# A four-block transformer kernel on one core: moving the context-maximum steps, a pair's low parts and one table load inside the first two stages

## The chip, the cores and the metric

The kernel runs as one launch on one core of a Trainium2 chip. The metric is the device time of that core in microseconds (us). Three runs of the kernel before took 817.12, 817.11 and 817.55 us; the median is 817.12 us.

## What is computed

The input `x` is 4 batches of 512 tokens of 512 values (2048 tokens, sixteen tiles of 128). Four blocks follow each other, each a residual step over a layer norm:

```
x = x + matmul(quant_1x128(layernorm(x)), quant_128x128(ctx_2048))        # stage a
x = x + down(silu(gate(ln(x)) * gate_s) * (up(ln(x)) * up_s)) * down_s    # stage b, inner size 1408
x = x + softmax_attention(ln(x), ctx_2048, mask)                          # stage c
x = x + ternary FFN with Hadamard transforms and 8-bit rounding           # stage d, inner size 2048
```

For stage a both operands are rounded to 8-bit floats and scaled back. The context of each batch is a 512x512 matrix in sixteen 128x128 blocks; each block has one scale, which comes from the largest absolute value in the block:

```
amax = max(abs(wb), over the block);  safe = maximum(amax, 1e-6)
q = (wb * (448 / safe)).astype(float8_e4m3fn);  wdq = q * (safe / 448)
```

## The kernel before

Stages a and b run together. The sixteen tiles go in eight pairs ("groups" g = 0 to 7). In group g TensorE runs stage b's gate and up products for the pair 2g, 2g+1 in eleven chunks c = 0 to 10 (`C0`), of 16 matmuls of 128x256 each (`gate_up_b`, L1340). Between the chunks, at chunk numbers that are written out by hand, stand the steps of stage a for the next pair, n0 = 2g+2 and n1 = 2g+3: `a_turn` (four transposes of the quantized tile, L1307) and `a_product` (eight fp32 matmuls with the context, L1312). After the chunks come `b_down(2g)`, the turns of the next pair's normed tiles (`b_turn`), and `b_down(2g+1)`. ScalarE and VectorE have `b_group` functions of their own, with the same chunk numbers. Each engine runs its own list in the order written; semaphores alone tie the engines together.

The steps that the change touches:

- A chunk's hidden values: ScalarE `b_silu` (L503) waits for the chunk; VectorE `b_hidden` (L922) waits for the silu; ScalarE `b_high` (L509) and VectorE `h_low` (L929) split the result in two fp16 parts. Chunk n of TensorE waits for `b_hidden` of chunk n-2 (`wait(pe, b_h_r, n - 1)`, L1342), since two PSUM banks take turns.
- Stage a for tile j: ScalarE `a_scale` (L468), VectorE `a_grids` and `a_rounding`, ScalarE `a_back` (L476, writes what `a_turn` turns), TensorE `a_turn`, ScalarE `a_evac` (L484), TensorE `a_product`, VectorE `a_residual`.
- The context of batch e (e = 1, 2, 3; batch 0 is done ahead of the groups): `context_max(e)` on VectorE (L789, one reduce of 128x2048), `max_turn(e)` on TensorE (L1322, one transpose into PSUM bank 2), `context_top(e)` on VectorE (two small operations, L793), `max_spread(e)` on TensorE (L1329, spreads the sixteen maxima over all partitions), `context_scales(e)` on VectorE (L799), then four times `context_scaled` on ScalarE (L449, four ACTIVATEs each), `context_grid` and `context_rounding` on VectorE (two operations each), and `context_back` on ScalarE. `context_scaled(e, b)` waits for `context_scales(e)`. Batch 1 is handled in groups 0 and 1, batch 2 from group 1 on, batch 3 from group 3 on.
- At a group's end: ScalarE copies the turned tiles out (`b_evac(n0)`, `b_evac(n1)`, L497), VectorE subtracts to get their low parts (`b_low`, L869). TensorE's next group waits for both low parts (`pe.wait_ge(b_xl_r, 2 * g + 2)`, L1364). VectorE's `b_down(2g)` (L945) is the scaling of the down product and the residual addition, two operations of 128x512.
- The first `Silu` on ScalarE stands at group 0, chunk 0.

The next stages, c and d, follow on TensorE behind group 7; stage c's context loads wait for `a_add`, stage d's weight loads for `b_add` and for their roundings.

Of the kernel before, what the change touches and what calls it, by code (L numbers as in the profile page):

```python
# [5 lines left out]
T, D, B, S2 = 2048, 512, 4, 512  # L6
# [19 lines left out]
def fused_blocks(nc, x, ctx_t, ctx_n, mask, gate_t, up_t, down_t, gate_s, up_s, down_s,  # L26
# [4 lines left out]
    ACT = mybir.ActivationFunctionType  # L31
# [3 lines left out]
    with ExitStack() as ctx:  # L35
# [411 lines left out]
        def _(act):  # L447
# [68 lines left out]
            def b_group(g):  # L516
                n0, n1, more = 2 * g + 2, 2 * g + 3, g + 1 < PAIRS
                odd, e, following = g % 2 == 1, (g + 2) // 2, (g + 3) // 2
                sums = (0, 0, 3, 5, 8, 10, 13, 16)
                for c in range(C0):  # L520
                    b_silu(g, c)
                    if c >= 1:
                        b_high(g, c - 1)
                    if more:
                        if c == 2:
                            a_back(n0)
                        if c == 4:
                            a_evac(n0)
                            a_scale(n1)
                        if c == 7:  # L530
                            a_back(n1)
                        if c == 8:
                            a_evac(n1)
                        if g == 0 and 6 <= c < 10:
                            context_scaled(1, c - 6)
                        if g == 1 and c in (3, 5):
                            context_back(1, 2 + c // 5)
                        if g in (3, 5) and c == 0:
                            context_back(e, 3)
                        if c in (0, 6, 9):  # L540
                            k = sums[g] + (0, 6, 9).index(c)
                            if k < sums[g + 1]:
                                weight_sums(k)
                    elif c == 6:
                        act.wait_ge(valid_ps, 1)
                        nc.scalar.activation(valid[:, :], bank(2)[:, 0:B], ACT.Copy).then_inc(valid_r, 1)
                b_high(g, C0 - 1)
                if more:
                    if odd and following < B:
                        for b in range(KD):  # L550
                            context_scaled(following, b)
                    elif g in (2, 4):
                        for b in range(3):
                            context_back(e, b)
                    elif g == 0:
                        context_back(1, 0)
                    if n0 + 2 < NT:
                        a_scale(n0 + 2)
                    b_evac(n0)
                    b_evac(n1)  # L560
                    if g == 0:
                        context_back(1, 1)
# [17 lines left out]
            nc.scalar.activation(ds_bc[:, :], bank(7), ACT.Copy).then_inc(ds_r, 1)  # L580
            a_evac(1)
            a_scale(2)
            b_evac(0)
            b_evac(1)
            act.wait_ge(row_in, 64)
# [179 lines left out]
        def _(dve):  # L765
# [187 lines left out]
            def b_group(g):  # L953
                n0, n1, more = 2 * g + 2, 2 * g + 3, g + 1 < PAIRS
                odd, e, following = g % 2 == 1, (g + 2) // 2, (g + 3) // 2
                for c in range(C0):
                    if c == 0 and g:
                        b_down(2 * g - 1)
                    b_hidden(g, c)
                    if c >= 1:  # L960
                        h_low(g, c - 1)
                    if more:
                        if c == 0:
                            a_grids(n0)
                        if c == 1:
                            a_rounding(n0)
                        if c == 2:
                            a_stats(n1)
                        if c == 3:
                            a_norm(n1)  # L970
                        if c == 5:
                            a_grids(n1)
                        if c == 6:
                            if g == 0:
                                context_scales(1)
                            a_rounding(n1)
                        if c == 7:
                            a_residual(n0)
                            b_stats(n0)
                        if c == 9:  # L980
                            b_norm(n0)
                        if g == 0:
                            if c == 2:
                                context_max(1)
                            if c == 4:
                                context_top(1)
                            if c == 8:
                                context_grid(1, 0)
                            if c == 10:
                                context_grid(1, 1)  # L990
                                context_rounding(1, 0)
                        elif g == 1 and c in (2, 4):
                            context_rounding(1, 1 + c // 2)
                        elif not odd and e < B:
                            if c in (4, 6, 8):
                                context_grid(e, c // 2 - 2)
                                context_rounding(e, c // 2 - 2)
                        if odd and following < B:
                            if c == 6:
                                context_max(following)  # L1000
                            if c == 9:
                                context_top(following)
                        if g == 6 and c == 6:
                            mask_rows()
                    elif c == 2:
                        weight_scales()
                h_low(g, C0 - 1)
                if odd and following < B:
                    context_scales(following)
                if more:  # L1010
                    a_residual(n1)
                    b_stats(n1)
                    if n0 + 2 < NT:
                        a_stats(n0 + 2)
                    b_norm(n1)
                    if n0 + 2 < NT:
                        a_norm(n0 + 2)
                    if g == 0:
                        context_rounding(1, 1)
                        dve.wait_ge(ds_r, 1)  # L1020
                    elif not odd and e < B:
                        context_grid(e, 3)
                    b_low(n0)
                    b_down(2 * g)
                    b_low(n1)
                    if g == 0:
                        context_grid(1, 2)
                        context_grid(1, 3)
                    elif not odd and e < B:
                        context_rounding(e, 3)  # L1030

            for g in range(PAIRS):
                b_group(g)

# [262 lines left out]
        def _(pe):  # L1297
# [63 lines left out]
            def b_group(g):  # L1361
                n0, n1, more = 2 * g + 2, 2 * g + 3, g + 1 < PAIRS
                odd, following = g % 2 == 1, (g + 3) // 2
                pe.wait_ge(b_xl_r, 2 * g + 2)  # L1364
                for c in range(C0):
                    gate_up_b(g, c)
                    if more:
                        if c == 4:
                            a_turn(n0)
                        if c == 6:  # L1370
                            if g == 0:
                                max_spread(1)
                            a_product(n0)
                        if c == 8:
                            a_turn(n1)
                        if c == 10:
                            a_product(n1)
                        if g == 0 and c == 4:
                            max_turn(1)
                        if odd and following < B and c == 8:  # L1380
                            max_turn(following)
                        if odd and following < B and c == 9:
                            max_spread(following)
                    elif c == 4:
                        pe.wait_ge(mask_r, 2)
                        M(bank(2)[:, 0:B], one_f, vrow[:, :], start=True, stop=True).then_inc(valid_ps, 1)
                if g == 0:
                    pe.wait_ge(dn_in, 16)
                    pe.wait_ge(ds_r, 1)
                b_down(2 * g)  # L1390
                if more:
                    b_turn(n0)
                    b_turn(n1)
                else:
                    c_body(-1, 1)
                b_down(2 * g + 1)
# [282 lines left out]
```

## Time and profile before

| what | value |
|---|---|
| median of three runs | 817.12 us |
| the profiled execution, its own time | 815.84 us |
| its span in the trace | 814.0 us (1.84 us lie around it) |
| TensorE busy | 733.8 us, 90% of the span |
| VectorE busy | 609.0 us, 75% |
| ScalarE busy | 421.4 us, 52% |
| GpSimd busy | 261.5 us, 32% |
| mean granted TensorE clock | 0.98 of full |

Rows of the trace give a start in us from the span's start, a duration in us, the engine and line, the operation with what it writes and reads, the count, and in brackets how long the engine stood idle before it and what ended that wait. PE is TensorE (PEld its weight loads), DVE is VectorE, ACT is ScalarE, POOL is GpSimd, SP the engine that issues loads. The groups of stage b begin in the trace at 46.28, 90.58, 133.06, 171.42, 215.53, 253.88, 293.39 and 331.74 us.

### The profile page before, as it was taken

What the parts mean: (1) busy time and instruction counts of PE and PEld (TensorE: products, weight loads), DVE (VectorE), ACT (ScalarE), POOL (GpSimd) and SP (SyncE); (2) the same over time, 40 slices, a digit from 0 to 9 for tenths busy, and PEclk for the clock granted to TensorE, in tenths of its full rate; (3) what the DMA queues carried; (4) which work ended last, traced back from release to release, by engine and by line L of the source; (5) the groups of instructions that cost most, each with busy time, mean ns of one, the idle gap of its engine ahead of it and who ended that gap; (6) DMA issues with size and microseconds to landing.
All of it is one profiled execution on the core that took longest, in us unless ns stands there. A gap on an engine that the chain in (4) does not pass through costs nothing. (4 is left out here: it accounts for less than half of the span.)

```text
span 814.0 us, 13263 instructions
## 1 busy us (share of the span) xinstructions
PE 733.8 (90%) x4443; PEld 449.2 (55%) x4480; DVE 609.0 (75%) x1308; ACT 421.4 (52%) x930; POOL 261.5 (32%) x164
## 2 busy tenths in 40 slices
PE   1579989998999999999999999769999999999947
PEld 0256656666666676754444444345656556555644
DVE  6667877976697677455878865987887888887864
ACT  3536566655665645322122123345777666677645
POOL 3000100000000000000000000498888788888840
PEclk9989999999999999999999999999999999999969
DMA  8950122112111211742333200000000000000001
GB/s 195 268 219 1 40 74 95 40 39 79 31 49 40 78 40 30 282 138 103 122 114 143 103 1 0 1 0 15 14 14 14 13 14 26 13 13 13 14 13 40
DMA packets 24646, 51.71 MB, mean 64 GB/s; under 512 B 2066, under 2 KB 4114, under 8 KB 23572
## 3 DMA queue, kind: packets, MB, share of 16 engines
q1 hardware_dynamic: 21684, 45.96, 16.7%
q0 software_dynamic: 2480, 4.33, 3.0%
q10 hardware_dynamic: 432, 0.79, 0.3%
q8 instruction: 28, 0.46, 0.2%
q14 instruction: 22, 0.18, 0.1%
HBM read 51.20 MB, written 4.19 MB: 68 GB/s over the span
## 5 line engine op out<-in xcount | busy, mean ns | idle before, releaser
L1346 PE MATMUL ps<-arena 128*128 128x256 f16 x1408 | 165.8, 277 | 7.0 <-DVE arena L926 3.4
L1346 PEld LDWEIGHTS ps<-arena 128*128 128x128 f16 x1408 | 137.7, 99 | 35.1 <-DVE arena L926 9.1
L1469 PE MATMUL ps<-arena 128*128 128x512 bf16 x484 | 117.2, 379 | 5.2 <-DVE arena L1122 3.6
L406 POOL TENSOR_TENSOR arena<-arena 128x1024 f32<-128x1024 f32 x42 | 101.5, 2416 | 40.8 <-DVE arena L1131 37.6
L1303 PE MATMUL ps<-I,arena 128*128 128x128 f32 x576 | 82.1, 284 | 31.9 <-ACT arena L481 15.1
L407 POOL TENSOR_TENSOR arena<-arena 128x1024 f32<-128x1024 f32 x42 | 101.1, 2406 | 0.0
L1303 PEld LDWEIGHTS ps<-I,arena 128*128 128x128 f32 x576 | 69.2, 146 | 57.2 <-issue 22.1
L354 POOL TENSOR_TENSOR rstd_a<-ve_a,mhalf 128x1 f32<-128x1 f32 x32 | 19.6, 611 | 250.2 <-DVE ve_a L777 244.0
L354 POOL TENSOR_TENSOR rstd_b<-ve_b,mhalf 128x1 f32<-128x1 f32 x32 | 17.6, 550 | 204.8 <-DVE ve_b L777 204.8
L507 ACT ACTIVATE arena<-ps,gs 128x256 f32<-128x256 f32 x88 | 41.1, 467 | 80.0 <-PE ps L1346 80.0
L926 DVE SCALAR_TENSOR_TENSOR arena<-ps,us,arena 128x256 f32<-128x256 f32 x88 | 42.3, 480 | 51.1 <-ACT arena L507 50.9
L1357 PE MATMUL ps<-arena 128*128 128x512 f16 x352 | 78.6, 379 | 0.0
L1469 PEld LDWEIGHTS ps<-arena 128*128 128x128 bf16 x512 | 48.7, 98 | 52.3 <-issue 2.7
L1122 DVE SCALAR_TENSOR_TENSOR arena<-ps,f_sm,arena 128x512 f32<-128x512 f32 x64 | 48.0, 750 | 34.4 <-ACT arena L637 33.4
L637 ACT ACTIVATE arena<-ps,f_sm 128x512 f32<-128x512 f32 x64 | 44.0, 688 | 47.8 <-PE ps L1469 47.6
L1319 PE MATMUL ps<-arena 128*128 128x512 f32 x128 | 60.3, 616 | 0.8 <-issue 0.8
L1415 PE MATMUL ps<-arena 128*128 (+1 forms) x128 | 59.2, 605 | 0.0
L1555 PE MATMUL ps<-arena 128*128 128x512 bf16 x247 | 56.9, 379 | 2.2 <-ACT arena L662 1.7
L1357 PEld LDWEIGHTS ps<-arena 128*128 128x128 f16 x352 | 34.4, 98 | 41.9 <-issue 4.0
L1430 PE MATMUL ps<-arena 128*128 (+1 forms) x128 | 57.5, 592 | 0.0
L606 ACT ACTIVATE arena<-ps,c_sm 128x512 f32<-128x512 f32 x16 | 11.0, 688 | 85.3 <-DVE c_sm L1063 85.3
L656 ACT ACTIVATE arena<-ps 128x512 f32<-128x512 f32 x56 | 30.4, 600 | 34.8 <-PE ps L1534 34.7
(128 smaller groups left out, 1184.3 us busy)
## 6 DMA issues: line engine op xcount, KB each, us to landing
arena<-in_ctx_t SPq DMA_DIRECT2D x7, 1024.0 KB, 5.3
arena<-in_wg_t SPq DMA_DIRECT2D x16, 256.0 KB, 3.4
arena<-in_wu_t SPq DMA_DIRECT2D x16, 256.0 KB, 4.0
arena<-in_wd_t SPq DMA_DIRECT2D x16, 256.0 KB, 4.1
arena<-in_ctx_n SPq DMA_DIRECT2D x4, 1024.0 KB, 7.5
arena<-in_wg_t SPq DMA_DIRECT2D x4, 1024.0 KB, 5.0
arena<-in_wu_t SPq DMA_DIRECT2D x4, 1024.0 KB, 4.8
arena<-in_wd_t SPq DMA_DIRECT2D x4, 1024.0 KB, 5.2
```

Of the source, the lines that this page charges most:

```text
L406: nc.gpsimd.tensor_tensor(b[:, :, 0, :], a[:, :, 0, :], a[:, :, 1, :], ALU.add).then_inc(d_bfp, 1)
L407: nc.gpsimd.tensor_tensor(b[:, :, 1, :], a[:, :, 0, :], a[:, :, 1, :], ALU.subtract).then_inc(d_bfp, 1)
L637: nc.scalar.activation(d_sil[n % 2], bank(2 * (n % 2)), ACT.Silu, scale=f_sm[:, u, 4:5]).then_inc(d_sil_r, 1)
L1122: V.scalar_tensor_tensor(HA[u][:, D * n:D * n + D], bank(2 * (n % 2) + 1), f_sm[:, u, 5:6], d_sil[n % 2], ALU.mult, ALU.mult).then_inc(d_h ...
L1303: last = nc.tensor.transpose(dst[:, b, :], src[:, b * P:b * P + P], eye_sb)
L1319: last = M(bank(5), a_xT[u][:, b, :], wdq[:, e % 2, b, :], start=(b == 0), stop=(b == KD - 1))
L1346: last = M(bank(n % 2)[:, 2 * P * i:2 * P * i + 2 * P], W[:, b, c * P:c * P + P], part[:, b, at:at + 2 * P], start=(b == 0 and part is xhT ...
L1357: last = M(bank(6 + j % 2), part[:, c, at:at + P], dW[:, c, :], start=(c == 0 and part is hh), stop=(c == C0 - 1 and part is hl))
L1415: last = M(bank(2 + u), c_xT[u][:, b, :], ctxs[:, bass.ds(B - 1 - e, 1), 0, b, :].rearrange("p a m -> p (a m)"), start=False, stop=(b == K ...
L1430: last = M(bank(6 + w), c_pT[w][:, b, :], ctxs[:, bass.ds(B - 1 - e, 1), 1, b, :].rearrange("p a m -> p (a m)"), start=(b == 0), stop=(b = ...
L1469: last = M(bank(2 * (n % 2) + i), d_qT[u][:, b, :], W[:, b, D * n:D * n + D], start=(b == 0), stop=(b == KD - 1))
L1555: last = M(bank(down_bank(j)), yqT[:, c, :], Wd[:, c, :], start=(c == 0), stop=(c == C1 - 1))
```

## The change

Six things are changed, all in the order of work; no arithmetic is added but one dummy `Silu` over one column.

1. `context_max(1)` stands ahead of group 0 on VectorE, instead of in chunk 2.
2. The rest of batch 1's chain in group 0 comes earlier: `max_turn` at chunk 0 (was 4), `max_spread` at 2 (was 6, ahead of `a_product`), `context_top` at 0 (was 4), `context_scales` at 2 (was 6), `context_scaled` at chunks 3, 5, 6, 9 (was 6 to 9), `context_grid(1, 0)` at 4 (was 8), `context_rounding(1, 0)` at 8 (was 10).
3. `a_turn(n1)` on TensorE and `a_evac(n1)` on ScalarE stand at chunk 9 instead of 8, in groups 0 to 6.
4. In groups 1 and 3 `max_spread(following)` stands at chunk 10, behind `a_product(n1)`, instead of at chunk 9.
5. `b_low(n1)` on VectorE stands directly behind `b_low(n0)`, ahead of `b_down(2g)`.
6. A `Silu` over one column into `b_sil[0]` stands ahead of ScalarE's `b_evac(0)`, with its wait for the small loads.

```diff
--- before.py
+++ after.py
@@ -529,10 +529,10 @@
                             a_scale(n1)
                         if c == 7:
                             a_back(n1)
-                        if c == 8:
+                        if c == 9:
                             a_evac(n1)
-                        if g == 0 and 6 <= c < 10:
-                            context_scaled(1, c - 6)
+                        if g == 0 and c in (3, 5, 6, 9):
+                            context_scaled(1, (3, 5, 6, 9).index(c))
                         if g == 1 and c in (3, 5):
                             context_back(1, 2 + c // 5)
                         if g in (3, 5) and c == 0:
@@ -580,6 +580,8 @@
             nc.scalar.activation(ds_bc[:, :], bank(7), ACT.Copy).then_inc(ds_r, 1)
             a_evac(1)
             a_scale(2)
+            act.wait_ge(row_in, 64)
+            nc.scalar.activation(b_sil[0][:, 0:1], gs[:, 0:1], ACT.Silu)
             b_evac(0)
             b_evac(1)
             act.wait_ge(row_in, 64)
@@ -971,8 +973,6 @@
                         if c == 5:
                             a_grids(n1)
                         if c == 6:
-                            if g == 0:
-                                context_scales(1)
                             a_rounding(n1)
                         if c == 7:
                             a_residual(n0)
@@ -980,15 +980,16 @@
                         if c == 9:
                             b_norm(n0)
                         if g == 0:
+                            if c == 0:
+                                context_top(1)
                             if c == 2:
-                                context_max(1)
+                                context_scales(1)
                             if c == 4:
-                                context_top(1)
+                                context_grid(1, 0)
                             if c == 8:
-                                context_grid(1, 0)
+                                context_rounding(1, 0)
                             if c == 10:
                                 context_grid(1, 1)
-                                context_rounding(1, 0)
                         elif g == 1 and c in (2, 4):
                             context_rounding(1, 1 + c // 2)
                         elif not odd and e < B:
@@ -1021,14 +1022,15 @@
                     elif not odd and e < B:
                         context_grid(e, 3)
                     b_low(n0)
+                    b_low(n1)
                     b_down(2 * g)
-                    b_low(n1)
                     if g == 0:
                         context_grid(1, 2)
                         context_grid(1, 3)
                     elif not odd and e < B:
                         context_rounding(e, 3)
 
+            context_max(1)
             for g in range(PAIRS):
                 b_group(g)
 
@@ -1368,18 +1370,18 @@
                         if c == 4:
                             a_turn(n0)
                         if c == 6:
-                            if g == 0:
-                                max_spread(1)
                             a_product(n0)
-                        if c == 8:
+                        if g == 0 and c == 2:
+                            max_spread(1)
+                        if c == 9:
                             a_turn(n1)
                         if c == 10:
                             a_product(n1)
-                        if g == 0 and c == 4:
+                        if g == 0 and c == 0:
                             max_turn(1)
                         if odd and following < B and c == 8:
                             max_turn(following)
-                        if odd and following < B and c == 9:
+                        if odd and following < B and c == 10:
                             max_spread(following)
                     elif c == 4:
                         pe.wait_ge(mask_r, 2)
```

## Rows read from the trace of the kernel before

**Rows 1.** The page: busy time and share of each engine.
```profile
PE 733.8 (90%) x4443; PEld 449.2 (55%) x4480; DVE 609.0 (75%) x1308; ACT 421.4 (52%) x930; POOL 261.5 (32%) x164
```
**Rows 2.** Busy time in stretches: start:end, length, engines, granted clock, DMA share, GB/s.
```profile
46.20:420.00 373.80, 358.40 (x2173) 233.80 (x2173) 271.26 (x625) 189.09 (x537) 22.15 (x37) 0.99 0.25 81
```
**Rows 3.** TensorE's waits: line, releaser: total us, times, longest us.
```profile
PE ps L1303 <- ACT arena L481: 15.1, 9, 9.7
...
PE ps L1331 <- DVE cmx_diag L797: 5.4, 3, 2.3
...
PE ps L1346 <- DVE arena L926: 3.4, 5, 1.0
...
PE ps L1346 <- DVE arena L872: 2.5, 2, 1.5
```
**Rows 4.** Timeline of TensorE in group 0 and at the start of group 1.
```profile
59.24 0.28 PE L1327 MATMUL ps<-I,cmx 128*16 128x128 f32 x1 [1.00 <-DVE cmx L791]
...
61.95 1.92 PE L1346 MATMUL ps<-arena 128*128 128x256 f16 x16 [0.40 <-DVE arena L926]
...
71.60 0.66 PE L1303 MATMUL ps<-I,arena 128*128 128x128 f32 x4 [0.28 <-ACT arena L481]
...
90.58 9.18 PE L1346 MATMUL ps<-arena 128*128 128x256 f16 x80 [1.02 <-DVE arena L872]
```
**Rows 5.** Timeline of VectorE in group 0.
```profile
51.73 0.48 DVE L926 SCALAR_TENSOR_TENSOR arena<-ps,us,arena 128x256 f32<-128x256 f32 x1 [5.60 <-ACT arena L507]
...
56.92 2.27 DVE L791 TENSOR_REDUCE cmx<-arena 128x16 f32<-128x2048 f32 x1
```
**Rows 6.** The issue of batch 1's context load on SP's queue.
```profile
26.18 0.40 SPq L292 DMA_DIRECT2D arena<-in_ctx_t  x1
```
**Rows 7.** All three context loads of L292: from issue to landing.
```profile
DMA to landing us min/median/max: 7.7/10.3/11.9
```
**Rows 8.** A stretch of group 0, columns as in rows 2.
```profile
52.00:54.00 2.00, 2.00 (x21) 1.80 (x19) 1.85 (x6) 0.78 (x2) 0.00 (x0) 1.00 0.15 51
```
**Rows 9.** Timeline of ScalarE around group 0's start.
```profile
42.28 0.60 ACT L501 ACTIVATE arena<-ps 128x512 f16<-128x512 f32 x1 [7.65 <-PE ps L1303]
...
49.93 1.28 ACT L507 ACT_TABLE_LOAD   x1 [4.52 <-PE ps L1346]
```
**Rows 10.** Timeline of VectorE at group 0's end.
```profile
80.45 0.68 DVE L859 TENSOR_TENSOR X<-X,ps 128x512 f32<-128x512 f32 x1
...
89.84 0.68 DVE L872 TENSOR_TENSOR arena<-ps,arena 128x512 f16<-128x512 f32 x1
```
**Rows 11.** Timeline of TensorE in groups 1 and 3.
```profile
117.18 0.39 PE L1331 MATMUL ps<-cmx_diag,ones 16*128 16x16 f32 x2 [2.32 <-DVE cmx_diag L797]
117.50 1.92 PE L1346 MATMUL ps<-arena 128*128 128x256 f16 x16
119.26 3.60 PE L1319 MATMUL ps<-arena 128*128 128x512 f32 x8
...
197.97 0.39 PE L1331 MATMUL ps<-cmx_diag,ones 16*128 16x16 f32 x2 [2.32 <-DVE cmx_diag L797]
198.29 3.44 PE L1346 MATMUL ps<-arena 128*128 128x256 f16 x16
```
**Rows 12.** A stretch of group 3, columns as in rows 2.
```profile
199.00:200.00 1.00, 1.00 (x6) 0.72 (x5) 0.00 (x0) 0.00 (x0) 0.00 (x0) 0.50 0.47 117
```
**Rows 13.** Timeline of ScalarE at group 1's end.
```profile
121.77 4.78 ACT L454 ACTIVATE arena<-arena,cinv 128x128 f32<-128x128 f32 x16 [0.86 <-DVE cinv L803]
128.51 1.28 ACT L473 ACTIVATE arena<-arena,a_sm 128x128 f32<-128x128 f32 x4 [1.97 <-DVE a_sm L839]
```
**Rows 14.** The same stretch on VectorE.
```profile
132.24 0.68 DVE L872 TENSOR_TENSOR arena<-ps,arena 128x512 f16<-128x512 f32 x1
```
**Rows 15.** Stage d: TensorE's two longest waits.
```profile
549.42 3.60 PE L1452 MATMUL ps<-H,arena 128*128 128x512 f16 x8 [5.28 <-DVE arena L1104]
...
782.96 1.94 PE L1303 MATMUL ps<-I,arena 128*128 128x128 f32 x8 [8.14 <-DVE arena L1192]
```

## The prediction

> **What bounds the kernel now.** I read the busy shares first [rows 1]: TensorE is the fullest engine, 90%. That is a mean over four stages, so I took the stretch that the change touches, from group 0's start to the end of stage b [rows 2]: of 373.80 us TensorE works 358.40. At most 15.4 us of waiting can be had there, plus what a lowered clock costs; VectorE (271.26) and ScalarE (189.09) have room on average. Then TensorE's waits by releaser [rows 3], and the timeline, to place each. Inside groups 0 to 7 they are few: waits for `a_back` at the second turn of each pair, for `context_top` at `max_spread`, for `b_hidden` at a chunk, for the low parts at a group's start, and once for `context_max`. As TensorE is otherwise back to back, each microsecond of wait removed there moves everything behind it, unless something else is late next.
>
> **Batch 1's maxima, group 0.** `context_max(1)` holds VectorE from 56.92 for 2.27 us [rows 5]. Behind it TensorE stands 1.00 us at `max_turn`, and 0.40 us at chunk 6, whose `b_hidden` is queued behind the reduce [rows 4]. Ahead of group 0 VectorE stands idle 5.60 us before its first `b_hidden` at 51.73 [rows 5]; the reduce takes 2.27 of these, so it costs nothing if the context has landed. Its load was issued at 26.18 [rows 6] and the slowest of the three such loads took 11.9 us [rows 7]: landed by about 38.5 (26.18 + 0.40 + 11.9), 7.6 us before VectorE gets there at 46.1. The loosest bound is the end of the traffic, which has ebbed by 52 [rows 8]; landing only then would hold back the first `b_hidden` by some 52 + 2.3 - 51.7 = 2.6 us. I take zero, as the landing row is the load's own.
> `max_turn` at chunk 0 finds the maxima made (about 48.4, against a chunk that ends at 49.9, when the first silu's wait ends [rows 9]). `max_spread` at chunk 2 finds `context_top` done: VectorE has it behind `b_hidden(0,0)` and `a_grids`, about 52.3, and chunk 2, which can't begin before that `b_hidden` ends at 52.2, ends after 54. Both small matmuls were there before. The clock is still at its lower level near 50, as it returns to 1.00 only in the stretch from 52 [rows 8]; the turn's 0.28 us may grow by 0 to 0.28, and I estimate 0.1, since part of it is latency.
> Next in line on VectorE is `b_hidden(0,3)`. Without the reduce it follows at about 57.3 instead of 59.11 (0.45 us of `context_scales` now stand in between), before chunk 5 wants it near 59. On ScalarE `context_scaled(1,0)` now stands in chunk 3: four ACTIVATEs, 4.78/4 = 1.2 us [rows 13]. It must not hold up silu 4; by my step-by-step list it ends at 58.9 and the chunk's matmuls at 58.8, so it costs 0.1 of a margin near 1 us. The later ones (chunks 5, 6, 9) stand beside chunks of 1.84 us (9.18/5 [rows 4]) or an `a_product` of 3.60 [rows 11]. Gain: 1.00 + 0.40 - 0.1 = 1.3 us. Bounds: 1.4 if all is hidden; -1.2 if the context is as late as the loosest bound.
>
> **The second turn one chunk later.** The 0.28 us of group 0 [rows 4] come back as 0.29 in each of groups 1 to 6 (seven rows of one pattern): `a_turn(n1)` arrives before `a_back(n1)` has ended. With a chunk of 1.84 us in between the wait goes: 0.28 + 6 x 0.29 = 2.0 us. Chunk 9 starts earlier instead; its `b_hidden` (chunk 7) was ready. Late next is the product behind chunk 10: it wants `a_evac(n1)`, queued on ScalarE behind silu 9 and `b_high` 8. Turn, silu, copy and evacuation are about 1.5 us after chunk 9, the product comes after turn and chunk 10, some 2.3 us. The weight sums are queued behind the evacuation, so silu 10 comes up to 0.6 later, and the last chunk's parts are wanted only at the end of `b_down(2g)`, over 5 us on. In groups 2 and 4 chunk 10 is within 0.1 us of its `b_hidden`. Bounds: 0 to 2.0; I take 2.0.
>
> **The spread behind the product, groups 1 and 3.** TensorE waits 2.32 us at 117.18 and at 197.97 [rows 11] for `context_top`, which VectorE can't start before chunk 9's `b_hidden`. Now chunk 10 and the product, over 5 us, lie in between: 2 x 2.32 = 4.64. Queued behind the wait were chunk 10, the product and `b_down`; now only `b_down` is, and the maxima are made 3 us earlier. In group 3 the wait was followed by half speed: chunk 10 took 3.44 us, in group 1 1.92 [rows 11], and the granted clock was 0.50 [rows 12], the lower of the two levels. That is 1.52 more. Bounds: 0 (it was not the wait) to 1.52; I take it whole, since the fall comes right after the idle stretch.
> What this makes late is `context_scales`, thus `context_scaled`: it began at 121.77, 0.9 before `b_down(2)` at 122.69 (behind the product [rows 11]), and will begin 0.6 after it, 1.5 us later against the matmuls. `a_scale` behind it had idled 1.97 for VectorE [rows 13], so this is hidden with 0.5 to spare. VectorE itself waits for the spread before `a_residual`, some 0.4 us more in its chain. Without its cover that would go 1:1 into the group start; the next edit gives the cover.
>
> **Low parts together.** In group 1 `b_low(n1)` runs 132.24 to 132.92 [rows 14], just ahead of the group start at 133.06. In group 0 it runs 89.84 to 90.52 [rows 10] and TensorE waits 1.02 [rows 4]. Putting it ahead of `b_down(2g)` saves two operations, 1.3 us, there. Group 0's end is helped twice: `context_rounding(1,0)` no longer stands ahead of `a_residual` at 80.45 [rows 10]. Gain 1.02 in group 0, 0 elsewhere, and it covers the 0.4 above. `b_down(2g)` lies 0.7 us later, TensorE waits for it only a group on. The price would be VectorE's backlog at group 1's start, where TensorE waits 0.70 + 0.39 in chunks 5 and 6 (in the 3.4 us of L926 [rows 3]); the list puts the first `b_hidden` 2.6 us behind the start (before, 2.8: 93.35 against 90.58). Bounds for the edit: 0 to 1.02; I take 1.02.
>
> **The table load.** It ran 49.93 to 51.21, and goes into the 7.65 us in which ScalarE waits before 42.28 [rows 9]. TensorE didn't wait for the first silu: no wait in the timeline before 57.65. Zero, between 0 and 1.28.
>
> **The sum.** 1.3 + 2.0 + 4.64 + 1.52 + 1.02 = 10.5 us (of the 3.4 us of waits for L926 [rows 3] only group 0's 0.40 goes; the other four stay). Stages c and d follow on TensorE; their loads wait for `a_add` and `b_add`, which come earlier by as much. The profiled execution took 815.84 (span 814.0); it becomes 805.3 (span 803.5). The median stands 1.28 higher than it; with the same distance the forecast is 806.6 us.
>
> **Rivals.**
> Clock by phase. The 2.32 us wait lowered the clock in group 3 and not in group 1, so more than the length of a wait decides. Everything behind group 0 now comes at other instants. The page "TensorE: Matmul & The Clock Gate" of the Trainium skill, section "What's actually happening", says that the window which decides runs free and doesn't start with the kernel; this trace's two groups agree with it, and by it a slow stretch may appear or vanish anywhere. One slow stretch like group 3's more is +1.5, two +3.0: 808.1 to 809.6. In stage d the stretches behind waits of 5.28 and 8.14 us [rows 15] can shrink or grow likewise, so -2 is possible too: 804.6. Chance of +1.5 or more: 0.12.
> The stall moves. `context_scaled` and the low parts end later than my list says, and TensorE loses at the starts of groups 2 and 4 what it won at the spread: 4.64 back, 811.2; with the slow clock kept in group 3, 812.8. For it: 0.14 us between `b_low` and the start before. Against: 1.3 us by the new order. Chance 0.07.
> Group 0 gives nothing: the context isn't there, or VectorE's list is the bound in groups 0 and 1. Without 1.3 and 1.02, 808.9. Chance 0.04.
> The change does nothing, because the chain in stage b has a cover that I don't see: 817. Against it: loads of c wait for `a_add`. Chance 0.03.
> Slower: stage d's filling. Its waits lie at 515 to 550 us, and TensorE's work there might fall under half clock. Work of 1 us costs 1 us more there, less the idle time that it fills. 27 us of work and 8 of idle lie between 510 and 545; all at half clock would be +19, so 825. It decides once over 10.5 + 8 = 18.5 us of that work is slow, four times what any slow stretch in front of it has. Chance 0.03.
>
> **How the numbers follow.** Forecast 0.71, with its own range 804.5 to 808.5. To leave no more than 2 in 10 outside: down to 803.5 (a shorter slow stretch in d), up to 810.5 (two slow stretches, or group 0 without gain). About 0.2% (1.6 us) can be told from no change. Faster: forecast, clock, moved stall, group 0, 0.94, lowered to 0.93; same 0.03; slower 0.04.
>
> **What would show it.** No wait at L1327 and L1331 in groups 0, 1 and 3; none of 0.29 at the second turn; chunk 10 of group 3 at 1.92; group 1 starting near 88.0, group 2 near 128, group 4 near 206. A wait on L872 at a group start means the stall moved. The prediction is wrong if the stretch of stage b shrinks by less than 8 us, or if stages c and d grow.

## The result and the profile after

The changed kernel takes 803.61 us (median of 5 runs, 802.32 to 804.72). The kernel before took 817.11 us beside it; the ratio is 0.9841, 95% interval 0.9827 to 0.9855. On another chip, later, it was 0.9855 (0.9835 to 0.9875). That is 12 to 13.5 us, where 10.5 were forecast; 803.61 lies 0.1 us inside the lower end of the range (803.5 to 810.5), and two of the five runs lie below it.

The busy shares and TensorE's waits of the changed kernel, to be laid beside [rows 1] and [rows 3]; the lines named here stand two further down than before (L1303 is L1305, L1327 is L1329, L1331 is L1333, L1346 is L1348, L926 is L928, L872 is L874):

```profile
PE 730.3 (91%) x4443; PEld 448.9 (56%) x4480; DVE 609.0 (76%) x1308; ACT 420.8 (52%) x931; POOL 261.5 (33%) x164
```
```profile
PE ps L1305 <- ACT arena L481: 13.1, 2, 9.7
...
PE ps L1348 <- DVE arena L928: 3.0, 4, 1.0
PE ps L1348 <- DVE arena L874: 1.5, 1, 1.5
...
PE ps L1333 <- DVE cmx_diag L799: 0.7, 1, 0.7
```
The seven waits at the second turn are gone (nine waits have become the two in front of the groups), so are both at the spread, the one at a group's start, and one of the five at a chunk; `context_max` no longer appears. TensorE's busy time falls by 3.5 us of the 12.2 that the span loses. That is no work saved: it is mostly the slow chunk of group 3, a quicker start of group 0, and short waits that lie inside the merged rows and have no bracket.

From the timelines of both kernels, the length of each group on TensorE, start to start:

| group | before | after | difference | forecast |
|---|---|---|---|---|
| ahead of group 0 | 46.28 | 45.92 | -0.36 | 0 |
| 0 | 44.30 | 39.87 | -4.43 | -2.6 |
| 1 | 42.48 | 39.58 | -2.90 | -2.6 |
| 2 | 38.36 | 38.27 | -0.09 | -0.3 |
| 3 | 44.11 | 39.55 | -4.56 | -4.1 |
| 4 | 38.35 | 38.28 | -0.07 | -0.3 |
| 5 | 39.51 | 39.01 | -0.50 | -0.3 |
| 6 | 38.35 | 38.17 | -0.18 | -0.3 |
| 7, to stage c's first product | 31.10 | 31.10 | 0.00 | 0 |
| the rest of the span | 451.16 | 452.05 | +0.89 | 0 |

They add up to the spans' difference, 814.0 - 801.8 = 12.2 us. The 0.89 us of the last row lie in stage d: from stage c's first product to the matmul behind stage d's 5.28 us wait both traces need 186.58 us. TensorE's timeline after, against [rows 4] and [rows 11]:

```profile
45.92 3.57 PE L1348 MATMUL ps<-arena 128*128 128x256 f16 x16 [1.50 <-DVE arena L874]
49.29 0.42 PE L1329 MATMUL ps<-I,cmx 128*16 128x128 f32 x1
...
53.37 0.39 PE L1333 MATMUL ps<-cmx_diag,ones 16*128 16x16 f32 x2
...
69.80 0.60 PE L1305 MATMUL ps<-I,arena 128*128 128x128 f32 x4
...
85.79 9.17 PE L1348 MATMUL ps<-arena 128*128 128x256 f16 x80
94.79 0.60 PE L1305 MATMUL ps<-I,arena 128*128 128x128 f32 x4
96.10 1.92 PE L1348 MATMUL ps<-arena 128*128 128x256 f16 x16 [0.71 <-DVE arena L928]
98.41 1.92 PE L1348 MATMUL ps<-arena 128*128 128x256 f16 x16 [0.39 <-DVE arena L928]
...
111.14 3.60 PE L1321 MATMUL ps<-arena 128*128 128x512 f32 x8
114.67 0.39 PE L1333 MATMUL ps<-cmx_diag,ones 16*128 16x16 f32 x2
114.99 4.92 PE L1359 MATMUL ps<-arena 128*128 128x512 f16 x22
...
147.35 0.60 PE L1305 MATMUL ps<-I,arena 128*128 128x128 f32 x4
148.07 1.92 PE L1348 MATMUL ps<-arena 128*128 128x256 f16 x16
...
187.21 1.91 PE L1348 MATMUL ps<-arena 128*128 128x256 f16 x16
```
Group 0's turn, spread and second turn start without a wait, and so does group 1. Group 1 keeps its two chunk waits. Chunk 10 of group 3, at 187.21, takes 1.91 us. In group 2 the turn at 147.35 is followed by a chunk 0.72 later, where group 1's start-to-start is 0.44 (108.95 to 109.39): 0.28 of hidden waiting, which has no bracket.

ScalarE and then VectorE of the same kernel, against [rows 9], [rows 13] and [rows 5]:

```profile
34.67 1.28 ACT L584 ACT_TABLE_LOAD   x1
...
56.52 1.28 ACT L454 ACTIVATE arena<-arena,cinv 128x128 f32<-128x128 f32 x4
57.70 0.45 ACT L507 ACTIVATE arena<-ps,gs 128x256 f32<-128x256 f32 x1
...
115.59 4.78 ACT L454 ACTIVATE arena<-arena,cinv 128x128 f32<-128x128 f32 x16 [2.01 <-DVE cinv L805]
121.03 1.28 ACT L473 ACTIVATE arena<-arena,a_sm 128x128 f32<-128x128 f32 x4 [0.66 <-DVE a_sm L841]
```
```profile
45.69 2.28 DVE L793 TENSOR_REDUCE cmx<-arena 128x16 f32<-128x2048 f32 x1
50.10 0.48 DVE L928 SCALAR_TENSOR_TENSOR arena<-ps,us,arena 128x256 f32<-128x256 f32 x1 [2.13 <-ACT arena L507]
...
83.07 1.29 DVE L874 TENSOR_TENSOR arena<-ps,arena 128x512 f16<-128x512 f32 x2 [0.59 <-ACT arena L501]
```
The context had landed: the reduce starts the moment VectorE is free and 2.13 us of idle time are left behind it. The first `context_scaled`, at 56.52, is followed by the silu without a wait. Both low parts of group 0's end run together at 83.07 and are done 1.4 us before group 1 starts. The scaling of batch 2 begins 0.60 us after `b_down(2)` (115.59 and 114.99), as forecast, and `a_scale` behind it still waits 0.66 for VectorE; 0.5 was the margin named.

### The profile page after: what moved, and what is told of

The parts are those of the page before. It is cut to its first block and busy times, and to the rows that moved or that the text cites. A ratio compares the mean times of both kernels' runs of the same rounds, so it can differ in the third digit from the quotient of the medians.

```text
span 801.8 us, 13264 instructions
## 1 busy us (share of the span) xinstructions
PE 730.3 (91%) x4443; PEld 448.9 (56%) x4480; DVE 609.0 (76%) x1308; ACT 420.8 (52%) x931; POOL 261.5 (33%) x164
## 5 line engine op out<-in xcount | busy, mean ns | idle before, releaser
L1348 PE MATMUL ps<-arena 128*128 128x256 f16 x1408 | 163.9, 275 | 5.9 <-DVE arena L928 3.0
L1348 PEld LDWEIGHTS ps<-arena 128*128 128x128 f16 x1408 | 136.5, 98 | 33.6 <-DVE arena L928 9.7
L1305 PE MATMUL ps<-I,arena 128*128 128x128 f32 x576 | 82.7, 286 | 29.9 <-ACT arena L481 13.1
L1305 PEld LDWEIGHTS ps<-I,arena 128*128 128x128 f32 x576 | 70.3, 147 | 53.3 <-issue 22.1
L928 DVE SCALAR_TENSOR_TENSOR arena<-ps,us,arena 128x256 f32<-128x256 f32 x88 | 42.2, 480 | 38.5 <-ACT arena L507 38.4
```

What stands on the lines that cost most here:

```text
L1305: last = nc.tensor.transpose(dst[:, b, :], src[:, b * P:b * P + P], eye_sb)
L1348: last = M(bank(n % 2)[:, 2 * P * i:2 * P * i + 2 * P], W[:, b, c * P:c * P + P], part[:, b, at:at + 2 * P], start=(b == 0 and part is xhT ...
```

## The experiments

Each kernel is the kernel before, or the changed one, with one piece moved; further and further2 move more. The lengths of groups 0, 1 and 3 come from each kernel's timeline. Ratios are against the kernel before on the same chip, with its 95% interval.

| kernel | us | ratio | g0 | g1 | g3 |
|---|---|---|---|---|---|
| before (first trace) | 817.12 | 1 | 44.30 | 42.48 | 44.11 |
| b1_only | 812.63 | 0.9954 (0.9941 to 0.9967) | 40.95 | 42.46 | 44.05 |
| spread_only | 810.43 | 0.9929 (0.9916 to 0.9942) | 44.11 | 40.22 | 40.18 |
| low_only | 815.22 | 0.9990 (0.9981 to 1.0000) | 42.95 | 44.51 | 42.44 |
| turn_only | 815.24 | 0.9978 (0.9966 to 0.9990) | 44.18 | 43.15 | 43.17 |
| table_only | 814.42 | 0.9984 (0.9970 to 0.9998) | 43.97 | 42.49 | 44.06 |
| table_again | 815.49 | 0.9988 (0.9976 to 0.9999) | 43.53 | 42.48 | 45.59 |
| spread_g1 | 812.40 | 0.9949 (0.9935 to 0.9962) | 44.10 | 40.22 | 42.44 |
| changed | 803.61 | 0.9841 (0.9827 to 0.9855) | 39.87 | 39.58 | 39.55 |
| after_again | 803.41 | 0.9855 (0.9835 to 0.9875) | 39.56 | 39.58 | 39.55 |
| no_low | 804.30 | 0.9862 (0.9842 to 0.9882) | 40.08 | 39.70 | 39.67 |
| turn_back | 806.46 | 0.9871 (0.9856 to 0.9886) | 41.11 | 40.09 | 40.06 |
| further | 801.62 | 0.9820 (0.9803 to 0.9837) | 40.58 | 39.59 | 38.37 |
| further2 | 799.31 | 0.9786 (0.9773 to 0.9799) | 40.35 | 38.37 | 38.37 |

**Batch 1's chain alone (b1_only).** The kernel before with edits 1 and 2.

```diff
+            context_max(1)
             for g in range(PAIRS):
                 b_group(g)
...                                     # and edit 2's lines
```


> The kernel before with batch 1's chain moved alone: maxima ahead of group 0, turn, top, spread, scales, scaling and grids at the earlier chunks. Theory W (the gain is the waits that go, each worth its idle column plus some 0.1 to 0.2 us of restart): group 0 loses the 1.00 and the 0.40 us waits, and since the rounding no longer stands ahead of the residual at its end, also most of the 1.02 at group 1's start, although the low parts keep their old order: 2.4 to 3.0 us faster than before, 814 to 815 us. Theory P (part of the 13.5 us measured for the whole change is the phase at which the low clock begins, not work): 1.4 to 2.4 faster, and the first five chunks' speed differs between this trace and the one of before for no reason in the order. Group 3's wait of 2.32 us at the spread stays in this kernel; by W its next chunk is at the lower clock again (3.4 us), by P it may be at either.

3.6 us faster, more than either theory had. Group 3 kept its wait and its slow chunk (3.52 us). TensorE's start of group 1 in this kernel:

```profile
87.64 9.16 PE L1346 MATMUL ps<-arena 128*128 128x256 f16 x80
```
No wait, with the low parts in their old order: the 1.02 us of [rows 4] went with the chain. From the first turn to group 1's start it needs 29.17 us (58.47 to 87.64) against 32.93 before (57.65 to 90.58). The turn and the spread of batch 1 now lie ahead of that stretch; they take 0.53 (50.06 to 50.27, 54.65 to 54.97). So 3.76 - 0.53 = 3.23 us are what the three waits cost, whose idle columns say 2.42.

**The spread alone (spread_only), and in group 1 alone (spread_g1).**

```diff
-                        if odd and following < B and c == 9:
+                        if odd and following < B and c == 10:          # spread_only
+                        if odd and following < B and c == (10 if g == 1 else 9):   # spread_g1
                             max_spread(following)
```


> The kernel before with max_spread(following) behind the product in groups 1 and 3, nothing else. Theory W: both 2.32 us waits go, with 0.1 to 0.3 of restart each, and group 3's chunk 10 is back at 1.92 us from 3.44: 6.2 to 7.0 us faster, about 810.5. Rival (the slow clock in group 3 was not the wait's doing): 4.7 to 5.2 faster, and chunk 10 or another chunk of group 3 still at half speed. Rival (the stall moves, for want of the low parts' new order): the starts of groups 2 and 4 wait 0.3 to 1.3 us for L872, and the gain is 4 to 5.5.

> The kernel before with max_spread behind the product in group 1 alone; group 3 keeps its 2.32 us wait and comes 2.3 us earlier. Group 1 shortens by 2.3 us. If the low clock belongs to the wait and only its phase decides, group 3's chunk 10 takes 3.2 to 3.5 us or 1.92, and the time is 2.3 to 3.9 us under that of the kernel before. If the low clock belongs to a place in group 3 and not to the wait, it is there again, as in every other kernel that has it there.

spread_only is 5.8 us faster, between theory W (6.2 to 7.0) and the rival without the clock (4.7 to 5.2). Its trace decides: no chunk of group 3 is slow. Group 1 loses 2.26 us, group 3 3.93: the difference, 1.67, is the clock. No bracket stands at the starts of groups 2 and 4, but 0.12 us of the stall did move there: from the second down product to group 2's start it is 4.87 us (124.74 to 129.61), against 4.75 in the changed kernel (120.62 to 125.37). spread_g1 is 4.3 us faster, more than the 2.3 to 3.9 expected: group 3 kept its wait and not its slow clock. The rows at the spread and the chunk behind it, from spread_g1, low_only and turn_only:

```profile
195.23 0.39 PE L1331 MATMUL ps<-cmx_diag,ones 16*128 16x16 f32 x2 [2.32 <-DVE cmx_diag L797]
195.56 1.92 PE L1346 MATMUL ps<-arena 128*128 128x256 f16 x16
```
```profile
116.11 0.60 PE L1331 MATMUL ps<-cmx_diag,ones 16*128 16x16 f32 x2 [2.32 <-DVE cmx_diag L797]
116.65 3.26 PE L1346 MATMUL ps<-arena 128*128 128x256 f16 x16
...
198.77 1.92 PE L1346 MATMUL ps<-arena 128*128 128x256 f16 x16
```
```profile
116.28 0.41 PE L1331 MATMUL ps<-cmx_diag,ones 16*128 16x16 f32 x2 [1.88 <-DVE cmx_diag L797]
116.63 3.51 PE L1346 MATMUL ps<-arena 128*128 128x256 f16 x16
...
197.66 0.39 PE L1331 MATMUL ps<-cmx_diag,ones 16*128 16x16 f32 x2 [1.88 <-DVE cmx_diag L797]
197.98 3.20 PE L1346 MATMUL ps<-arena 128*128 128x256 f16 x16
```
The first is spread_g1, the second low_only (slow in group 1, not in 3), the third turn_only (slow in both). In the seven traces that have the wait (with spread_g1's one, thirteen waits, of 1.88 us in turn_only and 2.32 elsewhere) the clock fell at seven. In the seven traces without either wait the granted clock is 1.00 from 54 to 530 us. So the fall needs the wait, and the wait's length does not decide it. That its instant does is the reading that is left; no run sets the instant alone. Runs of one kernel differ likewise: of the 66 runs of the kernel before beside these experiments, the eleven with a mean granted clock of 0.983 took 814.0 to 815.7 us, the 26 with 0.978 or 0.979 took 816.3 to 817.9. The Trainium skill, "TensorE: Matmul & The Clock Gate", section "What's actually happening", says that the deciding window runs free of the kernel; the trace agrees, with the same 2.32 us followed by 1.92 or by 3.26 to 3.59 us.

**The low parts alone (low_only), and the changed kernel without them (no_low).**

```diff
                     b_low(n0)
+                    b_low(n1)
                     b_down(2 * g)
-                    b_low(n1)
```


> The kernel before with b_low(n1) ahead of b_down(2g), nothing else. Theory W: the 1.02 us wait at group 1's start goes and no other: 1.0 to 1.2 faster, 816.0. Rival (VectorE is the bound in the first chunks of group 1): the chunk waits of 0.70 and 0.39 us there grow by up to 1.0 together, and the time stays.

> The changed kernel with b_low(n1) back behind b_down(2g). By the prediction's step (1.02 us, and it covers the spread's lateness): 1.0 to 1.4 us slower than the changed kernel, with a wait on VectorE's L874 at the starts of groups 1, 2 and 4. Theory W, corrected by the trace with batch 1's chain moved alone, where no such wait was left although the low parts had their old order: 0 to 0.5 slower.

Alone, it is 1.0 us faster, with an interval that reaches no change. Group 0 loses 1.35 us, its wait of 1.02 among them. Group 1 is 2.03 us longer: 1.56 of it follow the wait at the spread (a slow clock there, where group 3's went), and 0.47 come ahead of its first product, from 89.04 to 103.90 against 90.58 to 104.97. Those 0.47 are the rival's part: TensorE's waits for L926 are six with 4.0 us in sum, against five with 3.4 [rows 3]. In the changed kernel the edit is worth 0.12 us in each of groups 1 and 3 (the stall that moved in spread_only), nothing in group 0 from its first turn on (28.60 us with it, 28.59 without), and nothing that the times can tell (804.30 against 803.41, intervals overlapping).

**The second turn alone (turn_only), and the changed kernel with it back (turn_back).**

```diff
-                        if c == 8:
+                        if c == 9:
                             a_turn(n1)      # and a_evac(n1) on ScalarE
```


> The kernel before with the second turn and its evacuation one chunk later, nothing else. By the prediction's step 2.0 us faster. Theory W, corrected by the trace of the changed kernel: 0.3 to 0.5 in groups 0, 1, 3, 5 and 0.2 in group 6, nothing in groups 2 and 4, where chunk 10 then waits for its b_hidden: 1.4 to 2.2 faster. Rival (the silu of the last chunk, now behind the weight sums, is late for the down product): a wait at L1357 and less than 1 us of gain.

> The changed kernel with a_turn(n1) and a_evac(n1) back at chunk 8. By the idle column (0.28 + 3 x 0.29 in groups 0, 1, 3, 5, and next to nothing in 2, 4 and 6, where another wait had come in): 1.2 us slower. Theory W (each such wait costs 0.5 to 0.6 from start to start, its restart included; 0.1 to 0.2 in groups 2, 4, 6): 2.3 to 2.8 us slower, with groups 1 and 3 each 0.6 longer than in the changed kernel.

turn_only is 1.0 us faster, under both expectations (2.0, and 1.4 to 2.2). In its trace group 0 gains nothing from its first turn on (32.92 us against 32.93), as new waits of 0.15 and 0.18 us stand behind the turn. In groups 1 and 3 TensorE comes to the spread 0.95 us earlier, but in group 1 the clock fell behind the wait, which took 1.62 back.

With the turn back at chunk 8 the kernel is 10.2 us under the kernel before on its chip, where the changed one was 12.5 under on another: 2.3 us, though the ratios' intervals overlap. The traces carry it better: by groups it is 0.51 in each of 1, 3 and 5 and in group 0 from its first turn on (29.11 against 28.60), 0.07 in 2 and 4, 0.18 in 6. A bracket of 0.29 is worth 0.51. TensorE's matmuls of turn_back in group 1, and then its weight loads:

```profile
110.30 0.66 PE L1305 MATMUL ps<-I,arena 128*128 128x128 f32 x4 [0.29 <-ACT arena L481]
110.79 0.27 PE L1329 MATMUL ps<-I,cmx 128*16 128x128 f32 x1
```
```profile
110.30 0.42 PEld L1305 LDWEIGHTS ps<-I,arena 128*128 128x128 f32 x4 [0.57 <-ACT arena L481]
```
The two chunks ahead of the turn start at 106.35. In the changed kernel the same two are followed by the next start 3.49 us on (103.61 to 107.10); here it is 3.95, 0.46 more, and the turn itself takes 0.49 to the next start instead of 0.44. Much of the gap between bracket and price is in how rows are drawn: in the changed kernel the chunk at 109.39 has a row of 1.91 us, but the next row starts 1.75 after it, at 111.14, without a wait. A bracket is counted from the row's end, and so says about 0.16 us too little. The weight load's bracket, 0.57, is the nearer to the price.

**The table load alone, twice (table_only, table_again).**

```diff
+            act.wait_ge(row_in, 64)
+            nc.scalar.activation(b_sil[0][:, 0:1], gs[:, 0:1], ACT.Silu)
             b_evac(0)
```


> The kernel before with the one-column Silu ahead of b_evac(0), nothing else. By the prediction's step: no change, 0 to 0.3 us. Rival (the first silu's lateness holds back chunk 2, and so the clock's rise in group 0): 0.5 to 1.3 faster. Phase (the low clock of the waits in groups 1 and 3 comes or stays away, 1.5 us each): the trace may differ from before by up to 3 us in groups 1 and 3 with no wait changed.

> The same kernel as table_only once more, to see whether its 1.5 us (ratio 0.9984, interval 0.9970 to 0.9998) stand, since no wait of TensorE changed in its trace. Prediction's step: no change, a ratio of 0.9990 to 1.0005. Rival (the earlier first silu is worth something that the waits don't show, in the first chunks of group 0): 0.9980 to 0.9987 again.

Both times the kernel is faster by 0.1 to 0.2%, with intervals that end just under 1. No wait of [rows 3] changed in either trace. But spread_only, which has the table load at its old place, shows what it can cost:

```profile
45.28 5.35 PE L1346 MATMUL ps<-arena 128*128 128x256 f16 x32 [1.50 <-DVE arena L872]
51.28 5.41 PE L1346 MATMUL ps<-arena 128*128 128x256 f16 x48 [0.64 <-DVE arena L926]
```
There the clock rose earlier (two chunks in 5.35 us), and chunk 2 stood 0.64 us for the first `b_hidden`, which the load had held back: it runs 5.46 us after the group's start, in table_only 4.18:

```profile
50.44 0.48 DVE L928 SCALAR_TENSOR_TENSOR arena<-ps,us,arena 128x256 f32<-128x256 f32 x1 [4.32 <-ACT arena L507]
```
From group 0's start to its first turn, less what batch 1's turn and spread take there, the six traces with the load at its old place need 11.37 us (before), 11.26 (turn_only) and four times 11.25, never less. With the load ahead it is 11.05 (table_only), 10.60 (table_again), 10.74 (changed), 10.45 (after_again) and 10.95 to 11.46 in the other four. So the late `b_hidden` sets a floor of 11.25 us: 6.00 to chunk 2 (45.28 to 51.28), and 5.25 for three chunks at full clock (to 56.53). Only spread_only shows the stall with a bracket. The edit takes the floor away, and is worth nothing to 0.8 us by the instant at which the clock rises. What is left of the 0.9 to 1.5 us by the medians is open.

**The changed kernel again (after_again), and a further version (further, further2).**

```diff
# further, on the changed kernel; VectorE, group 0:
+                            if c == 6:
+                                context_grid(1, 1)
+                                context_grid(1, 2)      # was behind the group
-                            if c == 10:
-                                context_grid(1, 1)
+                            if c == 10:
+                                context_rounding(1, 1)      # was behind the group
# ScalarE:
-                        if g in (3, 5) and c == 0:
+                        if g in (3, 5) and c == 3:
                             context_back(e, 3)
# VectorE: b_stats(n0) in chunk 8 instead of 7 in groups 2, 4, 6
# further2: context_rounding(1, 2) at group 0's end instead of group 1's chunk 2
```


> The changed kernel itself beside the others on one chip, to have all differences from the same runs: 803 to 805 us, 12 to 14 less than the kernel before.

> The changed kernel with three more moves: batch 1's grids 1 and 2 in chunk 6 of group 0 and its rounding 1 in chunk 10 (0.85 us less of VectorE's work ahead of group 1's first chunk), context_back(e, 3) of groups 3 and 5 in chunk 3 instead of 0 (silu 1 no longer behind it), and b_stats(n0) in chunk 8 instead of 7 in groups 2, 4, 6 (chunk 10 no longer waits for its b_hidden). Theory W: waits of 0.71 and 0.39 in group 1 shrink by 0.8 together, 2 x 0.95 and 3 x 0.28 go, each with up to 0.2 of restart: 3.0 to 4.4 us faster than the changed kernel, near 800. Rival (VectorE's list, full in groups 2 and 4, makes the end of the group late instead): half of it.

> The kernel with three more moves, where group 1 kept its waits of 0.71 and 0.40 us: since its silu 1, behind the weight sums, and not VectorE's backlog set the start of the chain. Here context_rounding(1, 2) also moves from chunk 2 of group 1 to group 0's end, so 1.3 us of work go out of that chain. Theory: both waits go, group 1 takes 38.2 to 38.5 us instead of 39.59, and the time is 1.1 to 1.4 under the first version, 800.3 us. Rival (context_rounding(1, 2) makes the first b_hidden late): group 1 stays at 39.6 or grows.

further is 1.8 us under the changed kernel beside it, where 3.0 to 4.4 were expected. It saves 1.18 us in group 3, 1.16 in 5, and 0.3 in each of 2, 4 and 6, but nothing in group 1: VectorE now idled in front of the second `b_hidden` for silu 1, which is queued behind the weight sums, so the backlog I had cut was not the bound. Taking work out behind that point did it. VectorE in further:

```profile
92.52 0.48 DVE L928 SCALAR_TENSOR_TENSOR arena<-ps,us,arena 128x256 f32<-128x256 f32 x1 [0.92 <-ACT arena L507]
```
and TensorE in further2, where no `b_hidden` wait is left in stage b:

```profile
86.43 9.22 PE L1351 MATMUL ps<-arena 128*128 128x256 f16 x80
95.48 0.60 PE L1308 MATMUL ps<-I,arena 128*128 128x128 f32 x4
95.92 3.85 PE L1351 MATMUL ps<-arena 128*128 128x256 f16 x32
```
It takes 799.31 us, 17.4 less than the kernel before on its chip. further's 1.8 us are less than the 3.2 that its groups 2 to 6 saved; in its trace group 0 came 1.4 to 2.1 us later and its first chunks stood under the low clock longer.

## Why the prediction was right, and where it was small

**The bound and the forecast's sign.** Right: every wait that was to go went, TensorE closed up, and stage c and the first part of d moved with it (group 7 is equal to the hundredth). One sign of being wrong that the prediction named did come, small: stage d grew by 0.89 us behind its 5.28 us wait. Groups 1, 2 and 4 started at 85.79, 125.37 and 203.19, 2 to 3 us ahead of the 88.0, 128 and 206 named.

**Batch 1's chain, forecast 1.3, and the low parts, forecast 1.02.** Together 2.3; b1_only shows 3.23 for the chain alone. The step "gain 1.02 in group 0" for the low parts failed: the prediction itself said that group 0's end is helped twice, and the first help was enough. Of the 0.4 us that it was to cover it covered 0.12 in each of two groups.

**The second turn, forecast 2.0.** Measured 2.4: 0.51 in each of four groups, and next to nothing in 2, 4 and 6. The tight spot was named for 2 and 4 ("within 0.1 us of its `b_hidden`") and was yet counted whole; group 6 was not seen.

**The spread, 4.64.** Right: 2 x 2.26 in spread_only, 2 x 2.38 with the low parts as cover.

**The slow clock, 1.52.** Right in this pair of traces (1.67 by spread_only), and wrong as a size: the two waits draw a slow stretch in seven cases of thirteen, in group 1 as well as 3, one of them twice as dear: in table_again group 3 is 45.59 us, 3.15 above low_only's 42.44, as the product behind the slow chunk takes 4.91 us too, not 3.60. The trace that I priced it from holds one of them.

**What made the forecast small.** The term that was mis-sized is the price of the short waits: the idle column of the matmul row, taken 1:1. Start to start, 0.29 was 0.51, and 2.42 in group 0 were 3.23. The long wait at the spread was not dearer than its column, as the spread's place behind the product costs 0.10 us (from the product to the next start 3.53 us, not 3.43) and the stall 0.12. From group 0's first turn to group 7 the trace gains 12.1 us (less the 0.53 of the moved matmuls), 1.6 more than the 10.5 forecast: 1.0 in group 0 without its second turn, 0.3 at the turns, 0.15 each for the spread and the clock.

As idle time is under-read, the "at most 15.4 us" of the prediction are no ceiling either. From group 0 to stage c's first product TensorE is idle for 13.97 us before (316.56 less 302.59) and still for 1.78 in further2, yet that stretch is 16.70 us shorter there, of which the slow clock is 1.7.

The table load, put at nothing because no bracket stood before 57.65, is a second such term: the first five chunks took 11.37 us before and 10.74 after (in after_again 10.45), and 0.51 of these 0.63 us lie under the floor of the late `b_hidden`. That the clock rose early enough to give them is its phase, and luck. Another 0.36 us came ahead of group 0, which starts anywhere from 45.17 to 47.43 in the fourteen traces, for no cause that they show. Against these stand the 0.89 given back in stage d. That makes 12.2 us in all, between a trace of 815.84 and one of 803.61.

The last 1.3 us of the miss are the 1.28 that the forecast added because the median before stood so much over its trace. The changed kernel's trace is its median. The 1.28 are of the size of one slow stretch, which the changed kernel no longer has in stage b; that this is what they were is likely and not shown: no trace shows the 817.12 us run.

That 803.61 still lies in the range is luck: its lower end had been set for a shorter slow stretch in stage d, and stage d got longer.

**The rivals.** "The stall moves" and "group 0 gives nothing" fell: no wait at L874 behind group 0's, and the reduce ran at 45.69. Only 0.12 us a group of the stall moved, in spread_only. "Clock by phase" is borne out by seven falls in thirteen waits; the extra stretch did not come in stage b, since its waits had gone. "Slower" saw nothing: the rest of the span was 451.0 to 452.4 us in all fourteen traces.

## What to carry to other kernels

Price a wait by the interval from one start to the next, compared with the same pair of instructions elsewhere where they don't wait, not by the idle column: short waits of TensorE were worth about 0.2 to 0.3 us more than it, and one of 0.28 had no bracket at all. A step that always starts the same time behind another is a floor, also where no trace shows a wait at it: compare the stretch over several runs and look for a value that it never goes under. When two edits help the same wait, count it for the first and give the second nothing but its cover. After a wait is gone, look at what sets the start of the chain that is late, not at the length of the queue: in group 1 two waits stood until work behind the late silu was taken out.

## What was not expected of the hardware

The same 2.32 us wait for the same step was followed by a granted clock of 1.00 or by one of 0.50, the lower of the two levels, and at different groups in different kernels. Such a fall cost 1.6 to 1.7 us six times and 3.2 once, more than most edits here, so that one trace of each kernel can mislead by that much: low_only's trace shows 2.0 us more in group 1 and 1.7 less in group 3 than before, and all but 0.5 of both is the clock.
